# Two transformer blocks with conditioning: dense q and k tiles, modulation rows through DRAM, and maxima by twos in layer 0's attention

## The reference

```python
ada = silu(c) @ W_ada + b_ada                      # 6 rows of 288 for each batch item
shift_msa, scale_msa, gate_msa, shift_mlp, scale_mlp, gate_mlp = split(ada, 6, axis=-1)
h = layernorm(x) * (1 + scale_msa) + shift_msa
x = x + gate_msa * attention(h)                    # scale D ** -0.5, softmax
h = layernorm(x) * (1 + scale_mlp) + shift_mlp
x = x + gate_mlp * (gelu(h @ W_fc1 + b_fc1) @ W_fc2 + b_fc2)
```

## Time and profile before

| | us |
|---|---|
| median of 3 runs | 995.5 (993.51 to 996.24) |
| the profiled execution | 996.99 |
| its span | 995.2 |
| PE busy | 857.5 (86%) |
| DVE busy | 659.8 (66%) |
| ACT busy | 540.9 (54%) |
| POOL busy | 285.5 (29%) |

### The profile page before, as it was taken

The page is one execution under the profiler, slowest core; times in us unless marked ns, Lnnn a source line. Parts: engine busy times, 40 slices in busy tenths (PEclk is TensorE's granted clock), DMA queues, the critical chain, the costliest instruction groups (busy, mean ns, idle before and its releaser), DMA issues. The chain is left out here.

```text
span 995.2 us, 16869 instructions
## 1 busy us (share of the span) xinstructions
PE 857.5 (86%) x6204; PEld 387.7 (39%) x6204; DVE 659.8 (66%) x1278; ACT 540.9 (54%) x763; POOL 285.5 (29%) x339
## 2 busy tenths in 40 slices
PE   3798999999999999998887999995778874699996
PEld 1361122222222222222154646653445553455564
DVE  1868888888888888888068554553279768655521
ACT  1471577777777777777956324441456623355530
POOL 1512112223454421110045315223023446321222
PEclk9897799999999999999989999997899987799998
DMA  8000010111102100000500100001564540100000
GB/s 266 9 16 21 19 25 25 25 43 42 43 20 64 27 19 19 19 19 1 135 0 1 37 24 2 0 1 41 135 135 122 132 109 5 31 1 25 24 24 25
DMA packets 49615, 43.11 MB, mean 43 GB/s; under 512 B 23394, under 2 KB 40068, under 8 KB 49543
## 3 DMA queue, kind: packets, MB, share of 16 engines
q1 hardware_dynamic: 49543, 42.15, 16.2%
HBM read 25.45 MB, written 9.44 MB: 35 GB/s over the span
## 5 line engine op out<-in xcount | busy, mean ns | idle before, releaser
L816 DVE TENSOR_REDUCE row_max<-ps 128x1 f32<-128x512 f32 x512 | 324.5, 685 | 68.3 <-PE ps L1491 67.1
L1273 ACT ACTIVATE probs<-ps 128x1024 f32<-128x1024 f32 x256 | 248.5, 1017 | 45.2 <-PE ps L1518 44.9
L1491 PE MATMUL ps<-stack_area 54*128 54x512 f16 x512 | 161.3, 394 | 26.6 <-DVE row_max L816 21.2
L1530 PE MATMUL ps<-probs,mlp_area 128*32 128x512 f32 x1024 | 136.5, 605 | 0.5 <-ACT probs L1273 0.5
L1491 PEld LDWEIGHTS ps<-stack_area 54*128 54x128 f16 x512 | 40.4, 93 | 192.9 <-DVE row_max L816 172.1
L1518 PE MATMUL ps<-stack_area 56*128 56x512 f16 x512 | 110.2, 384 | 5.4 <-ACT probs L1273 5.1
L1616 PE MATMUL ps<-w_fc,mlp_area 128*128 128x288 f16 x864 | 108.9, 289 | 5.9 <-DVE mlp_area L939 5.9
L1603 PE MATMUL ps<-mlp_area,w_fc 128*128 128x512 f16 x504 | 110.4, 379 | 3.6 <-DVE v_sb L793 1.7
L1312 ACT ACTIVATE mlp_area<-ps 128x512 f32<-128x512 f32 x72 | 43.0, 597 | 116.3 <-PE ps L1603 115.3
L1616 PEld LDWEIGHTS ps<-w_fc,mlp_area 128*128 128x128 f16 x864 | 84.7, 99 | 29.4 <-DVE mlp_area L939 5.8
L625 POOL TENSOR_SCALAR neg_scaled<-neg_max 128x16 f32<-128x16 f32 x16 | 4.1, 254 | 277.5 <-DVE neg_max L823 277.5
(11 more groups left out here) (165 smaller groups left out, 1177.8 us busy)
## 6 DMA issues: line engine op xcount, KB each, us to landing
qkv_rows<-part_area SPq DMA_DIRECT2D x24, 252.0 KB
stack_area<-tokens SPq DMA_DIRECT2D x128, 36.0 KB
x_sb<-in_x SPq DMA_DIRECT2D x4, 576.0 KB, 14.1
stack_area<-part_area SPq DMA_DIRECT2D x64, 36.0 KB
w_raw<-in_L_cond_W_fc SPq DMA_DIRECT2D x4, 576.0 KB
w_raw<-in_L_cond_fc_w SPq DMA_DIRECT2D x4, 576.0 KB
tokens<-qkv_rows SPq DMA_DIRECT2D x64, 36.0 KB
v_sb<-qkv_rows SPq DMA_DIRECT2D x16, 144.0 KB
```

What stands on the lines that cost most here:

```text
L816: nc.vector.reduce_max(row_max[:, p % 2, t, j, half:half + 1], bank(bk), AX.X).then_inc(max_done, 1)
L1273: nc.scalar.activation(probs[:, n % 2, 2 * c:2 * c + 2, :].rearrange("p h n -> p (h n)"), ps[:, 2 + 2 * c:4 + 2 * c, :].rearrange("p b n - ...
L1491: nc.tensor.matmul(bank(bk), stacks[rows, p % RING, 0, t * P:(t + 1) * P], stacks[rows, p % RING, 1, half * 512:(half + 1) * 512], start=T ...
L1530: mm = nc.tensor.matmul(bank(6)[at:at + VW, :], v_pad[:, TB * (p // BPAIR) + n, 2 * (p % BPAIR) + j, :], probs[:, n % 2, 2 * c + j, :], st ...
```

## The change

It has five pieces.

1. The order of a slot on PE: maxima in twos. The third and fourth maximum products stand between the two halves of the scores, and in a slot with a part the first two stand together between the part's second and third product.
2. The q and k columns are stored densely (576 in the order q, k of head 0, q, k of head 1, ...), so seven fields of 18 make a tile of 126. There are five parts a batch item, ten in all, made ahead of the first pair that uses them; `store_stacks` takes its fields from one or two of them. The score scale moves into the exponent.
3. Modulation rows: `conditioning` contracts with 32 stationary columns (the two batch items repeated) and writes each of the six rows' places in its own group of 32 partitions, two places in round 0 and four in round 1. DVE scales the bias on these partitions and adds the product; rows 0 and 1 of each group are stored to a DRAM tensor and read back with a broadcast over the 128 partitions. In layer 0 ACT issues round 0's DMAs, SP the others; in layer 1 SP stores the rows after the first MLP chunk and reads them back in three steps (0 to 2 for attention, 3 and 4, and the gate 5).
4. Order of the start: half of the tokens, constants, weights, the other half, the rest of W_ada; statistics and inverse deviations in two halves; ACT scales the weights ahead of tile 0; value products lag six tiles; part 0's chunks come at tiles 6 and 10.
5. Weight jobs 3 and 4 of layer 1 move from the conditioning to the last MLP chunk of layer 0; job 2 stands alone after chunk 0.

```diff
+ADA_PLACES = ((0, 1), (2, 3, 4, 5))
+PG = P // D
+PROWS = PG * D
+BPARTS = -(-2 * H // PG)
+NPART = 2 * BPARTS
...
-        JOBS_AT_FC2 = (0, 2)
-        JOBS_AT_ADA = (1, 3, 5)
+        V_LAG, W_AT, ADA_AT, STAT_AT, RSTD_AT = 6, -1, 7, 3, 1
+        PARTS_AT, TAKES_AT = (6, 10), (8, 12)
+        JOBS_AT_FC2 = {0: (0, 2), 3: (0, 2)}
...
+        def part_place(p, x, j):
+            u, g = divmod(2 * (2 * (p % BPAIR) + j) + x, PG)
+            return BPARTS * (p // BPAIR) + u, D * g
+        def parts_used(p):
+            return sorted({part_place(p, x, j)[0] for x in range(2) for j in range(2)})
+        FIRST_PAIR = [min(p for p in range(NPAIR) if n in parts_used(p)) for n in range(NPART)]
...
-                if rest == 0 and 0 < p < NPAIR:
-                    return [("P", p, c)]
+                if rest == 0 and p > 0 and p in FIRST_PAIR:
+                    return [("P", FIRST_PAIR.index(p), c)]
...
+            def ada_round(l, r):
+                rows = slice(0, SW * len(ADA_PLACES[r]))
+                cols = ada_cols[rows, r, :]
+                dve.wait_ge(*ada_loads(l, r))
+                nc.vector.tensor_scalar(cols, cols, ada_plus[rows, r:r + 1], ada_factor[rows, r:r + 1], ALU.add, ALU.mult
+                                        ).then_inc(ada_scaled, 1)
+                dve.wait_ge(ada_scaled, 2 * l + r + 1)
+                dve.wait_ge(ada_mm, 2 * l + r + 1)
+                nc.vector.scalar_tensor_tensor(cols, bank(6 + r)[rows, 0:C], ada_factor[rows, r:r + 1], cols,
+                                               ALU.mult, ALU.add).then_inc(ada_sum, 1)
...
+            act.wait_ge(ada_sum, 1)
+            for g, place in enumerate(ADA_PLACES[0]):
+                nc.scalar.dma_start(ada_rows[0, :, place, :], ada_cols[SW * g:SW * g + B, 0, :]).then_inc(ada_stored, 16)
+            act.wait_ge(ada_stored, 16 * 2)
+            for b in range(B):
+                nc.scalar.dma_start(*spread_of(0, b, 0, 2)).then_inc(msa_in[b], 16)
...
                     project(part, 0, 2)
-                    side(maxima[0:1])
+                    side(maxima[0:2])
                     project(part, 2, 4)
-                    side(maxima[1:2])
-                    project(part, 4, 6)
                     side(other_of(s))
-                    project(part, 6, 7)
+                    project(part, 4, 7)
...
                         scores(*divmod(s + 1, SLOTS), 0)
-                    side(maxima[2:3])
+                    side(maxima[2:4])
                     if SCORES_FIRST <= s < NPAIR * SLOTS - 1:
                         scores(*divmod(s + 1, SLOTS), 1)
-                    side(maxima[3:4])
...
+            def conditioning(l, r):
+                pe.wait_ge(*ada_loads(l, r))
+                for k in range(3):
+                    for g, place in enumerate(ADA_PLACES[r]):
+                        mm = nc.tensor.matmul(bank(6 + r)[SW * g:SW * (g + 1), 0:C], silu_t[:, SW * k:SW * (k + 1)],
+                                              ada_w_sb[l][:, k, C * place:C * (place + 1)],
+                                              start=(k == 0), stop=(k == 2))
+                mm.then_inc(ada_mm, 1)
...
                 if l == 0:
-                    conditioning(1)
-                    pe.wait_ge(ada_sum, 4 * B * 2)
+                    pe.wait_ge(hT_ready[2], 8)
+                    for r in range(2):
+                        conditioning(1, r)
+                    pe.wait_ge(ada_sum, 4)
```

More of the change, by code:

```diff
@@ L185, in hidden_blocks_kernel @@
         const_in, const_ready = sem("const_in"), sem("const_ready")
-        x_in, cond_in, ada_in, fc2_bias_in = sem("x_in"), sem("cond_in"), sem("ada_in"), sem("fc2_bias_in")
+        x_in = [sem(f"x_in{q}") for q in range(4)]
+        cond_in, fc2_bias_in = sem("cond_in"), sem("fc2_bias_in")
+        ada_in = [sem(f"ada_in{r}") for r in range(2)]
         w_in, w_ready, w_step, w_scaled = sem("w_in"), sem("w_ready"), sem("w_step"), sem("w_scaled")
@@ L329, in hidden_blocks_kernel, with part_rows @@
         SCORES_FIRST = -1
+        def part_rows(n):
+            return min(PROWS, 2 * C - PROWS * (n % BPARTS))
+        def part_place(p, x, j):
[4 more added lines that the diff above has]
+        FIRST_PAIR = [min(p for p in range(NPAIR) if n in parts_used(p)) for n in range(NPART)]
+        PAIRS_OF = [[p for p in range(NPAIR) if n in parts_used(p)] for n in range(NPART)]
         def maxima_of(s):
@@ L356, in plan_banks @@
                 maxima, others = maxima_of(s), other_of(s)
-                for i, step in enumerate(part_of(s) + maxima[:2] + others + maxima[2:]):
+                for i, step in enumerate(part_of(s) + maxima[0:2] + others + maxima[2:4]):
                     now = s + i / 6
@@ L469, in _ @@
                     sp.dma_start(stacks[to:to + MR, i, 1, :], max_rows_sb[0:MR, :]).then_inc(k_ones, 16)
+            store_ada(0, 1)
+            for b in range(B):
+                spread_ada(0, b, 2, 6, late_in)
             store_stacks(0)
@@ L479, in _ @@
                     store_maxima(p + 1)
-            load_ada(1)
-            load_weights(1, 0, QKV_JOBS)
+            sp.wait_ge(part_mm, QC * NPART)
+            for r in range(2):
+                load_ada(1, r)
+            load_weights(1, 0, 1)
+            sp.wait_ge(lo_ready[1], NT)
+            for r in range(2):
+                load_ada_bias(1, r)
+            load_weights(1, 1, QKV_JOBS)
+            for r in range(2):
+                store_ada(1, r)
+            sp.wait_ge(h_ready[0], NT)
+            sp.wait_ge(proj_y, NT)
+            for b in range(B):
+                spread_ada(1, b, 0, 3, msa_in[b])
             load_weights(1, QKV_JOBS, HEAD_JOBS)
+            sp.wait_ge(h_ready[2], NT)
+            for b in range(B):
+                spread_ada(1, b, 3, 5, late_in)
             sp.wait_ge(fc2_y, NT)
@@ L485, in _ @@
                          ).then_inc(fc2_bias_in, 16)
+            sp.wait_ge(fc2_g, NT)
+            for b in range(B):
+                spread_ada(1, b, 5, 6, gate_in)
             load_weights(1, HEAD_JOBS, HEAD_JOBS + 1)
@@ L941, in mlp_chunk @@
                 if last and l == 0:
-                    scale_ada(1)
+                    for b in range(B):
+                        dve.wait_ge(msa_in[b], 32)
                     for t in range(2):
@@ L1060, in _ @@
                     for t in range(NT + 1):
+                        if t == STAT_AT:
+                            first_statistics(1)
+                        if t % TB == 0 and t < NT:
+                            dve.wait_ge(msa_in[t // TB], 16)
                         if t < NT:
@@ L1099, in _ @@
                 if l == 0:
-                    add_ada_bias(1)
+                    split_weights(1, 2)
+                    for r in range(2):
+                        ada_round(1, r)
                 with dve.Fori(1, 3) as c:
@@ L1224, in _ @@
             act.wait_ge(const_in, CONSTS)
-            for i in range(QKV_JOBS):
-                scale_weights(0, i)
             def high_part(ph, i, n, gap):
@@ L1324, in _ @@
                 if l == 0:
-                    for t in range(NT + 4):
-                        if t < NT:
+                    for t in range(W_AT, NT + V_LAG + 1):
+                        if 0 <= t < NT:
                             high_part(0, t % 2, t, 2 if t > 1 else 0)
@@ L1476, in value_mms, with part_mms @@
                 mm.then_inc(v_mm, 1)
-            def part_mms(p, c, bk, first, end):
-                t0 = L * (p // BPAIR) + 512 * c
+            def part_mms(n, c, bk, first, end):
+                t0 = L * (n // BPARTS) + 512 * c
+                row, rows = PROWS * (n % BPARTS), part_rows(n)
                 for i in range(first, end):
                     a, w = PRODUCTS[i]
-                    mm = nc.tensor.matmul(bank(bk), w_qk[:, w, p % BPAIR, :], hT_all[:, a, t0:t0 + 512],
+                    mm = nc.tensor.matmul(bank(bk)[0:rows], w_qk[:, w, row:row + rows], hT_all[:, a, t0:t0 + 512],
                                           start=(i == 0), stop=(i == len(PRODUCTS) - 1))
```

324 lines of the change are left out of this document (166 added, 158 removed).

## The result

978.3 us median (977.64 to 979.72) against 995.8 for the kernel before: ratio 0.983 (95% interval 0.981 to 0.985), faster by 17.5 us. The forecast was 968 us, with a range of 947 to 982. The profiled execution took 977.64 us (span 975.8), so its span is 19.4 us shorter than that of the kernel before. Of this, 2.4 us come up to the first maximum product, 5.6 in the loop between the first and the last copy of maxima, 9.6 in the middle. The other 1.8 us lie in the stretches around them (0.8 between the last copy and the end of the MLP's first chunk, 1.1 behind the second chunk's first products).

A forecast was written before the change was run, and what follows sets the result against it. The loop was held by waits between bank, reduction and product, no engine full; the lead-in by DVE. Start 10.2, loop 5.4, middle 12.0 and rest 0.4 sum to 28.0: 996.99 becomes 969, given as 968; range 947 to 982.

The forecast's parts named there:

- Start: Stretch up to the first maximum product: it comes at 66.3 us instead of 76.5, minus 10.2.
- rows at 19 to 21 us: At the start, modulation rows are back from the DRAM trip at 19 to 21 us; ends 18 and 28.
- 33.8 + 6.2: From first turn to first maximum: today's 33.8 us plus 6.2 for statistics, second conditioning round and later second chunk.
- The six-tile lag of the value products costs nothing: In the lead-in, lagging value products add 0 us, since they fill PE while pair 0's stacks travel.
- Loop, fewer parts and twos: Layer 0's attention loop: fewer parts save at most 14 us, the order by twos costs some back; together minus 5.4.
- from 2.49 to 2.71: Loop slots whose fourth maximum product waits for its bank grow by 0.22 us under the order by twos.
- Middle: Stop between the MLP's first two chunks at layer 1's conditioning: shorter conditioning and moved weight jobs give minus 12.0 us.
- Rest: Before layer 1 the gate copy of 576 columns goes, minus 0.4 us; dropping DVE's row scaling there gives 0.
- (B): Start hardly gains, 3 us instead of 10, from bulk loads or cold tiles: 975; chance 0.23 shared with another rival.
- (A): Order by twos costs nothing in the loop's slots, so it gains 20 us instead of 5.4: 953; chance 0.22.
- (C): Granted clock falls to 1.2 GHz in the loop, 1.4 us a slot, 1024 at 40 slots: slower; chance 0.05.
- (D): Paired maxima wait for both banks and still start apart, at most plus 5: 973; chance 0.23 shared with another rival.

The follow-up runs named there:

- e5: Changed kernel with SP holding its last 2.4 MB of bulk loads until the first modulation rows are back from DRAM: 971.9 us.
- e12: Changed kernel with value products five tiles behind instead of six, part 0's second chunk and ACT's takings earlier: 975.5 us.
- e4: Changed kernel with value products four tiles behind instead of six, part 0's chunks and ACT's takings one tile earlier: 977.9 us.
- e9: Changed kernel with DVE taking the second modulation sums at tile 9 instead of 7, PE's round left at tile 5: 977.6 us.
- e8: Kernel before with only the order of a slot changed, maxima in twos instead of single: 998.3 us, ratio 1.004.
- e1: Changed kernel with the slot's order of before, all four maxima single: 973.6 us.
- e2: Changed kernel with only the first two maxima of a slot together, the third and fourth split as before: 966.8 us.
- e3: Changed kernel with DVE making layer 1's modulation sums ahead of splitting weight job 2: 973.8 us.
- e7: Changed kernel with layer 1's conditioning rounds inside chunk 0's output products, sums ahead of job 2, only chunk 1's turns waiting: 974.3 us.
- e10: Changed kernel with conditioning rounds and DVE's sums inside chunk 0's output products, job 2 split behind chunk 1's first output tile: 968.8 us.
- e11: Changed kernel with only the first two maxima together, the last bulk loads held and the middle cleared of DVE's backlog: 953.3 us.

## Why the prediction was right and where it failed

The measured 978.3 lies in the stated range (947 to 982), but outside of the forecast's own range of 958 to 976: the range was wide enough because it took in the rivals, and that the number fell into it was in part luck. By the two traces, 28.0 us were forecast and 19.4 came. The start gave 7.8 less than its term and the middle 2.4 less; the loop gave 0.2 more and the rest 1.4 more.

**Start: sign right, size wrong.** Minus 10.2 was forecast for the first maximum, 2.4 was measured (the last section has the spread of this number). Of the 7.8 us between, 1.7 stand at the first turn (27.99 where 26.3 was forecast) and 6.1 behind it. Two terms failed.

The first is "rows at 19 to 21 us". They came at 25.3, inside the ends that I gave (18 and 28), but I took the value near the low end because the nearest row was a DMA in a quiet stretch, 2.2 us from issue to use. These DMAs run beside 6.8 MB of loads, and the row with bulk loads in it (11.0 us) was the one to go by. e5 shows the term: without the last bulk loads the rows come at 18.0 and the first turn at 23.96, even ahead of the 26.3.

The second is "33.8 + 6.2" behind the first turn. It measured 46.1 instead of 40.0. The first to the last normalisation take 6.6 us longer, where I had put down 4.7: the statistics take 3.8 us of DVE's time, as forecast, but the second round 0.9 and a wait of 0.7 for PE (1 was forecast), and DVE's waits for ACT's casts grow from 3.5 to 5.0. "The six-tile lag of the value products costs nothing" was wrong by some 2.3 us, of which about 0.9 are the lower clock: the issue of stack 0's last copy ends at 70.26, when PE still has value products until 72.2 and a part chunk of 2 us ahead of the first maximum. And the second chunk of part 0 came 3.3 us later against the tiles, not 1.5. e12 may have got a part of both back (not shown, see there), e4 and e9 did not.

**Loop, fewer parts and twos: right.** Forecast minus 5.4, measured minus 5.6. "23.8 a pair without a part" was 23.5, "25.7 with one" was 25.77 to 26.08 in the changed kernel and 25.70 in e8, "from 2.49 to 2.71" was 2.70. In slots with two side banks the weighing is 3.30 apart, with the output's copy 3.02, both as forecast. The mechanism is shown by e1, e2 and e8. One thing I worked out and did not use: the two couples of maxima could be judged apart, and the sum for the first couple was a gain (2.46 to 2.04 us a slot).

**Middle: right in mechanism, 2.4 short.** Minus 12.0 forecast, minus 9.6 measured. Job 2 started 2.9 us after chunk 0's end, where I had put 2.8, waiting for its last load. It took 3.0 us instead of 2.1, so chunk 1 came 8.0 behind instead of 6.6. The restart at 1.2 GHz cost 2.55, not 1.6; the 1.6 was a guess, and no row of the kernel before stood behind it or its bounds of 0 and 3.4. I named the wait for DVE and did not ask whether job 2 had to stand ahead of the sums; e3 shows that it had not.

**Rest.** 0.4 was forecast for the gate copy. It went, and the first turn of layer 1 came 0.7 us closer to the end of the products before it. The other 1.4 us by which the rest came out better are within the spread of these stretches.

**Rivals.** (B) is nearest, in mechanism as in time: the bulk loads held back the trip, the start gained 2.4 where B gave it 3, and the middle's 2.4 make up the rest to 978. But only a part of the start's missing gain is the trip's; the larger part was lost behind the first turn, as above. (A), that twos cost nothing, is false as they are ordered; its 20 us for the loop are nearly what e2 has (376.7 - 358.2 = 18.5). (C): the clock in the loop is 1.00 throughout. It fell in the lead-in, from 0.71 to 0.61, and that cost nothing there, where DVE is busy for 31.55 of 34.8 us: from the first maximum product to the first copy it is 22.4 us in both kernels. (D): both products of a couple start together at 426.51, so it falls. The ends of the range were rounded outwards: what is said to lie below A adds up to 947 and not 945, B and D together to 980 and not 982.

## What to carry to other kernels

Where two pieces of work are joined in an in-order queue, look at each junction by itself: here one saved 0.9 us a period and the other lost as much, and the sum of both looked like nothing. Price a small transfer through DRAM on the path at the start by a row with bulk loads beside it, and try to hold back those that are not needed yet. When a stop of an engine is removed, ask which other queue was catching up under it: PE's stop in the middle was only gone when DVE's backlog had a place of its own.

## What was not expected of the hardware

**Groups of columns run side by side.** The conditioning writes two places' products, or four, to separate groups of 32 partitions. At the start three steps of two places (12 records) took 3.10 us, and three steps of four places (24 records) took 3.10 as well (39.52 to 42.62). In the middle all six steps (36 records) took 3.10, so there a step runs at twice the pace. The clock column shows 1.00 for all three stretches and does not tell the early ones apart, though four transposes too took 0.59 us at the start (and 0.58 before, where the column shows 0.50) and 0.39 at 47.7 us. Why the column differs from the durations is open.

**A stationary tile of 126 columns loads more slowly than one of 128.** Groups by form, of before and of after (busy us, mean ns):

```profile
L1482 PEld LDWEIGHTS ps<-tokens 128*128 128x128 f16 x224 | 15.2, 99 | 42.7 <-DVE row_max L816 22.5 <-issue 15.0
```

```profile
L1578 PEld LDWEIGHTS ps<-tokens 128*126 128x126 f16 x112 | 13.9, 142 | 18.4 <-DVE row_max L886 10.1 <-issue 4.1
L1578 PEld LDWEIGHTS ps<-tokens 128*72 128x72 f16 x28 | 2.5, 112 | 5.5 <-DVE row_max L886 3.4 <-issue 0.9
```

142 ns against 99. The Trainium skill (TensorE: Matmul & The Clock Gate, Weight-path perf modes) says that the fast weight load is on only when there are 128 weights and the type is not fp32; this trace agrees. It may be the 0.2 us by which e1's pairs with a part stay above those of before; no run separates it.

**An operation of DVE can take several times as long beside one of POOL.** In the changed kernel a normalisation step took 2.38 us at 59.20, beside an operation of POOL that ran from 59.05 for 2.22 us, instead of 0.51; in the kernel before, the same pair took 2.38 and 2.22 at 64.03. In e4 it was 2.59 instead of 0.42 (above). Other steps beside POOL kept their time, and no run isolates the cause.

**The same code takes different times from execution to execution.** The changed kernel, e1, e2, e3, e7 and e10 have the same instructions up to the first maximum, which came at 70.90 to 74.23 us in their profiled executions (mean 73.1). The kernel before and e8 have it at 76.51 and 75.73, e5 and e11, which have the same start too, at 68.52 and 70.68. Windows of the changed kernel (74.09) and of e3 (70.90), columns as above:

```profile
60.00:66.00 6.00, 4.24 (x34) 2.66 (x33) 2.92 (x4) 2.47 (x6) 1.26 (x1) 0.80 0.13 33
66.00:71.00 5.00, 5.00 (x39) 3.81 (x37) 0.00 (x0) 2.61 (x6) 0.00 (x0) 0.89 0.16 48
```

```profile
60.00:66.00 6.00, 5.01 (x49) 3.88 (x50) 1.34 (x3) 3.72 (x8) 0.00 (x0) 1.00 0.18 46
66.00:71.00 5.00, 5.00 (x36) 3.48 (x34) 0.00 (x0) 2.06 (x6) 0.00 (x0) 1.00 0.12 37
```

The granted clock of 0.80 and 0.89 in one and 1.00 in the other goes with it. So the 2.4 us by which the first maximum moved between the two traces compared above are of the size of this spread; by the means it is about 3. Later stretches vary too: from the last copy of maxima to the output products of the MLP's first chunk it is 78.1 us in the changed kernel, 80.7 in e2 and e3, 77.7 in e10. The loop does not: in the changed kernel, e3, e7 and e10 its periods agree to 0.02 us from the second on. That is why the order of a slot is shown more firmly here than anything about the start.
